# Small matmuls of the identity in the idle places of TensorE between two attentions

## The chip, the cores and the metric

The kernel runs on one core of one Trainium2 chip. The metric is the device time of one execution in microseconds, as the median of several runs.

## What is computed

The reference runs two layers over 16 batches of 512 queries with 256 channels, with a context of 1601 rows. Layer 0 is a masked cross attention with 16 heads of 16, an output projection, a residual and a layer norm. Layer 1 is a Mamba-2 block followed by a second cross attention (8 heads of 32) over the same context.

```python
def reference(x, ctx_1024, mask_BxSxS2_ik1, mask_1xS2_bf0, ...):
    x = _L0_xattn_ref(x, ctx_1024, ctx_1024, mask_BxSxS2_ik1, ...)
    x = _L1_xattn_ref(x, ctx_1024, mask_1xS2_bf0, ...)
    return x

# the Mamba-2 block of layer 1
zxbcdt = _rms(x, norm_w) @ in_proj_w
z, xBC, dt = ...
dt = jax.nn.softplus(zxbcdt[..., -H_M:] + dt_bias)
conv = conv_b + sum((padded[:, k:k + L, :] * conv_w[:, k] for k in range(D_CONV)))
xBC = jax.nn.silu(conv)
...
def step(h, inp):
    dec, u, bt, ct = inp
    h = h * dec[:, :, None, None] + u[..., None] * bt[:, None, None, :]
    y = jnp.einsum('bhpn,bn->bhp', h, ct)
    return (h, y)
...
u = _rms(y.reshape(b, L, D_INNER) * jax.nn.silu(z), gnorm_w)
return resid + u @ out_proj_w
```

## The kernel before

All engines run a loop over the 16 batches, each with its own list of instructions written out by hand, and they meet through semaphores (`s_...`). TensorE's loop body is the one that the change touches. In the order of its queue, one batch is:

1. `group(b, g)` for the four groups of heads of layer 0: scores (L975, L977, L979), probabilities times values (L1004), and, between them, the raw scores (`entry`, L941) of the next group, from which VectorE takes row maxima.
2. The output projection of layer 0 (`project_out`, L1123), with projections of layer 1's keys and values in between. These come from a list, `SECOND`; `fill(n)` takes the next n of them and calls `project` (L903). They write banks 6 and 7 of PSUM.
3. A wait for the layer norm and the RMS norm, which VectorE and GpSimd compute. Then eight transposes of `xs` (L1140) into banks 0 and 1, `fill(1)`, and a wait for `xn`, which ScalarE copies from the transposes.
4. The projection into the Mamba block: L1158 gives dt (16 matmuls with 8 columns), L1164 gives the channels, each with 512 columns. ScalarE copies each result (`copy_raw`), VectorE convolves it (L1701, L1705), ScalarE takes tanh, VectorE gates. The first `copy_raw` calls stand ahead of the exponential that VectorE's softplus waits for. `whole_decays` (L1089, L1090) and `window_sums` (L1081) write bank 4, and banks 4 and 5.
5. The scan over four windows of 128 positions: L1183, L1187, L1192, L1197, L1211, L1214, L1222, with one `fill(1)` in each. Bank 5 is read last by ScalarE's exponential into `Ce`, counted by `s_Ecb`.
6. The output projection of the block (`project_block`, L1226), the sums of squares (L1237: 32 matmuls with one column), `fill(3)`. A wait for the next layer norm, eight transposes of `xs1` (L1248) into banks 2 and 3, a wait for `xn`, and layer 1's q projection (`LASTQ`, L903).
7. SyncE copies q1 to its place by DMA (L558) while the context of the next batch is being loaded (`load_ctx`, L524). TensorE waits for this copy, then computes the raw scores of layer 1 (`entry1`, L960), with the first projections of the next batch in between, and the two groups of heads of layer 1.

An f32 matmul appears in the trace as two records, a bf16 one as a single record. Each record has a weight load beside it (PEld).

`identb` is the identity matrix in bf16, `ident` in f32. `s_rawfree` counts the raw scores of layer 0 that VectorE has read (banks 4 and 5), `NCOUNT` of them for a batch.

Of the kernel before, what the change touches and what calls it, by code (L numbers as in the profile page):

```python
# [51 lines left out]
def xattn_mamba(nc, x, xt, ctxt, mask, maskt, mask1, wq0, bq0, wk0, bk0, wv0, bv0, wo0, bo0, ln_g, ln_b,  # L52
# [4 lines left out]
    QT = T // P  # L57
# [15 lines left out]
    NCOUNT = G0 * (RAW + 1)  # L73
# [8 lines left out]
    LEAD = 1  # L82
# [7 lines left out]
    with ExitStack() as ctx:  # L90
        def sb(name, shape, dt):
            return ctx.enter_context(nc.sbuf_tensor(name, shape, dt))

        def sem(name):
            return ctx.enter_context(nc.semaphore(name))
# [24 lines left out]
        identb = sb("identb", [P, P], BF16)  # L120
# [117 lines left out]
        ps = ctx.enter_context(nc.psum_tensor("ps", [P, 8, 512], F32))  # L238
# [35 lines left out]
        s_rawfree = sem("s_rawfree")  # L274
# [45 lines left out]
        s_Ecb = sem("s_Ecb")  # L320
# [89 lines left out]
        for kind, _, _ in ENTRIES:  # L410
            counted.append(counted[-1] + (kind in ("raw", "turn")))
# [9 lines left out]
        for cuts in CUTS:  # L421
            at_slot = {}
            for lo, hi, t0, t1 in cuts:
                n = (t1 - t0 + 1) * SLOTS
# [447 lines left out]
        def _(pe):  # L872
# [4 lines left out]
            def project(b, item, bank, before):  # L877

                layer, kind, i = item
                if before is None:  # L880
                    pass
                elif before == (0, "v", before[2]):
                    pe.wait_ge(s_projfree, b * KT + before[2] + 1)
                elif before == (1, "v", before[2]):
                    pe.wait_ge(s_vfree, b * KT + before[2] + 1)
                else:
                    pe.wait_ge(s_rest, rests(b, before) + 1)
                for k in range(DT):
                    if kind == "q":
                        o = ps[:, bank, 0:T]  # L890
                        l = (wq0_s, wq1_s)[layer][:, k, i * P:(i + 1) * P]
                        r = (xt_s, xn)[layer][:, k, :]
                    elif kind == "k":
                        c, w = KCH[i[1]]
                        o = ps[:, bank, 0:w]
                        l = (wk0_s, wk1_s)[layer][:, k, i[0] * P:(i[0] + 1) * P]
                        r = ctxs[:, k, c:c + w]
                    else:
                        rows = P if i < KT - 1 else LAST
                        o = ps[0:rows, bank, 0:D]  # L900
                        l = ctxs[:, k, i * P:i * P + rows]
                        r = (wv0_s, wv1_s)[layer][:, k, :]
                    mm = pe.matmul(o, l, r, start=(k == 0), stop=(k == DT - 1))  # L903
                mm.then_inc(s_proj, 1)
# [196 lines left out]
            with pe.Fori(0, B) as b:  # L1101
# [7 lines left out]
                pe.wait_ge(s_wl, 16 * NRELOAD * (b + 1))  # L1109
                second = list(SECOND)  # L1110

                def fill(n):
                    for _ in range(n):
                        k = len(SECOND) - len(second)
                        item = second.pop(0)
                        project(b, item, pj_bank[item], SECOND[k - 2] if k >= 2 else None)
# [11 lines left out]
                pe.wait_ge(s_p, (b * NG + G0) * KT * 2)  # L1128
                project_out(wo0_s, 0, G0 - 1, G0, G0 - 1)
                fill(1)  # L1130
                pe.wait_ge(s_norm, LEAD + b * NG + G0)
                project_out(wo0_s, G0 - 1, G0, G0)
                fill(1)
                fill(NC - 2 + V_LN)

                pe.wait_ge(s_y, QT * (b + 1))
                for i in range(QT):
                    pe.wait_ge(s_xs, b * QT + i + 1)
# [1 line left out]
                        mm = pe.transpose(ps[:, k, i * P:(i + 1) * P], xs[:, i, k * P:(k + 1) * P], ident[:, :])  # L1140
                mm.then_inc(s_xst, 1)
                fill(1)
                pe.wait_ge(s_xn, DT * (b + 1))

                for j in range(1 + NCH + XT):
# [9 lines left out]
                    if j == 0:  # L1155
                        for i in range(QT):
                            for k in range(DT):
                                mm = pe.matmul(ps[:, bank, i * HM:(i + 1) * HM], xn[:, k, i * P:(i + 1) * P],  # L1158
                                               win_s[:, k, 2 * DI + 2 * NS:2 * DI + 2 * NS + HM],
                                               start=(k == 0), stop=(k == DT - 1))  # L1160
                    else:
                        c0 = DI + CORDER[j - 1] * P if j <= NCH else (j - 1 - NCH) * P
                        for k in range(DT):
                            mm = pe.matmul(ps[:, bank, :], win_s[:, k, c0:c0 + P], xn[:, k, :],  # L1164
                                           start=(k == 0), stop=(k == DT - 1))
                    mm.then_inc(s_in, 1)
                fill(V_IN)
                for c in range(QT):
# [24 lines left out]
                    if c > 0:  # L1193

                        pe.wait_ge(s_Ld, nb + 1)
                        for e in range(2):
                            mm = pe.matmul(ps[:, 4 + e, :], ones[:, :], aU[:, 4 * e:4 * e + 4, :],  # L1197
                                           start=True, stop=True)
# [36 lines left out]
                for i in range(QT):  # L1235
                    for k in range(XT):
                        mm = pe.matmul(ps[:, 4, i:i + 1], zs[:, k, i * P:(i + 1) * P], ones[:, 0:1],  # L1237
                                       start=(k == 0), stop=(k == XT - 1))
                mm.then_inc(s_op, 1)
                project_block(QT - 1)  # L1240
                fill(3)
                assert not second

                pe.wait_ge(s_blk, QT * (b + 1))
                for i in range(QT):
                    pe.wait_ge(s_xs1, b * QT + i + 1)
                    for k in range(DT):
                        mm = pe.transpose(ps[:, 2 + k, i * P:(i + 1) * P], xs1[:, i, k * P:(k + 1) * P], ident[:, :])  # L1248
                mm.then_inc(s_xst1, 1)
                pe.wait_ge(s_xn1, DT * (b + 1))  # L1250
                for item in LASTQ:
                    project(b, item, pj_bank[item], None)
# [2 lines left out]
                def forward():  # L1255
# [5 lines left out]
                        pe.wait_ge(s_vfree, (b + 1) * KT)  # L1261
                    project(b + 1, item, pj_bank[item], FRONT[n - 2] if n >= 2 else None)

                pe.wait_ge(s_q1, (b + 1) * DT)
                for n in range(NENT1):
                    entry1(b, n)
# [566 lines left out]
```

## Time and profile before

| | |
|---|---|
| median of 3 runs | 9563.34 us (9562.64 to 9577.86) |
| profiled execution | 9599.96 us |
| its span | 9597.9 us |
| busy: TensorE, VectorE, ScalarE, GpSimd | 84%, 52%, 35%, 20% |
| mean granted clock of TensorE | 0.880 |

The span is the time from the first to the last instruction of the profiled execution. A granted clock of 1.00 is 2.4 GHz and 0.50 is 1.2 GHz; TensorE has one or the other, and a mean between them says how long it had each. One batch takes about 585 us, so every place in the loop occurs 16 times.

### The profile page before, as it was taken

How to read it: one execution, taken by the hardware profiler on the slowest of the kernel's cores; microseconds unless marked ns; L12 is line 12 of the kernel's file. 1: busy time of each engine (PE TensorE's matmuls, PEld its weight loads, DVE VectorE, ACT ScalarE, POOL GpSimd, SP SyncE). 2: the span in 40 equal slices, each digit the busy share in tenths (PEclk: the TensorE clock that was granted, in tenths of full speed). 3: DMA queues.
4: the chain of work that ended last, by engine and by line, in shares of the span. 5: the costliest groups of instructions: out<-in, count | busy, mean ns of one | idle time of the engine just before them, and what ended most of it. 6: DMA issues, size and time to landing. Idle time of an engine off the chain costs nothing.

```text
span 9597.9 us, 129251 instructions
## 1 busy us (share of the span) xinstructions
PE 8034.6 (84%) x38020; PEld 3528.0 (37%) x38020; DVE 5004.5 (52%) x12781; ACT 3321.4 (35%) x4038; POOL 1965.2 (20%) x1798
## 2 busy tenths in 40 slices
PE   3979889798887979879798897988879788897987
PEld 1333433334333343433334333343333433334343
DVE  3456354554545555454553545545455554545545
ACT  0424334242342414324143242423424244241432
POOL 3030220302213031130311303022030221303113
PEclk6989889898898989889798898988989899897988
DMA  4132231312303132131322313223131320313223
GB/s 79 20 61 34 40 57 19 67 28 41 61 14 68 27 57 48 20 66 22 64 39 37 60 19 61 34 40 57 19 68 27 50 55 12 70 24 59 45 28 60
DMA packets 216597, 421.47 MB, mean 44 GB/s; under 512 B 35542, under 2 KB 126584, under 8 KB 215812
## 3 DMA queue, kind: packets, MB, share of 16 engines
q1 hardware_dynamic: 215889, 412.67, 25.4%
q8 instruction: 367, 6.01, 0.3%
q14 instruction: 341, 2.79, 0.1%
HBM read 190.14 MB, written 8.51 MB: 21 GB/s over the span
## 4 chain that ended last, share of the span: by engine, by line
PE 61%; issue 12%; DVE 10%; POOL 6%; DMA 5%; ACT 3%; SPq 2%; DVEq 0%; POOLq 0%; ACTq 0%
PE ps L1004 13%; PE ps L941 10%; PE ps L975 7%; PE ps L977 7%; PE ps L903 6%; PE ps L1009 4%; PE ps L979 3%; PE ps L1123 3%; DMA stage<-in_mask 3%; DVE mx L1577 3%; POOL maskq L693 2%; PE ps L960 2%; PE ps L1040 2%; DMA qst<-q1hl 1%; DVE xc L1705 1%
## 5 line engine op out<-in xcount | busy, mean ns | idle before, releaser
L1354 ACT ACTIVATE PR<-ps 128x1024 f32<-128x1024 f32 x2496 | 2501.9, 1024 | 3009.2 <-PE ps L977 1629.4
L1548 DVE CUSTOM_DVE_ANT_0 ps<-ps,maskq 128x402 f32<-128x402 f32 x4203 | 2408.4, 587 | 1929.8 <-PE ps L941 1399.4
L1004 PE MATMUL ps<-PR,vbuf 128*32 128x512 f32 x9984 | 1358.8, 617 | 5.1 <-ACT PR L1354 5.1
L977 PE MATMUL ps<-maskk,identb 128*128 128x512 bf16 x3328 | 1276.0, 383 | 0.0
L941 PE MATMUL ps<-kst,qst 96*128 96x402 bf16 (+1 forms) x3115 | 1028.6, 343 | 86.9 <-DVE mx L1548 71.5
L979 PE MATMUL ps<-qst,kst 102*128 102x512 f32 x1664 | 769.8, 527 | 391.7 <-DMA qst<-mrow 320.9
L1577 DVE TENSOR_REDUCE mx<-ps 128x2 f32<-128x804 f32 x1024 | 932.9, 985 | 187.6 <-PE ps L960 186.9
L975 PE MATMUL ps<-qst,kst 99*128 99x512 bf16 x2496 | 958.2, 384 | 0.0
L960 PE MATMUL ps<-kst,qst 100*128 100x402 f32 x2048 | 761.2, 499 | 228.3 <-DMA qst<-q1hl 127.6
L709 POOL TENSOR_TENSOR khl<-rest,khl 128x402 fp32r<-128x402 f32 (+1 forms) x128 | 123.6, 965 | 3442.8 <-ACT rest L1320 3442.8
L941 PEld LDWEIGHTS ps<-kst,qst 96*128 96x128 bf16 x3115 | 282.9, 97 | 1192.3 <-DVE mx L1548 804.0
L960 PEld LDWEIGHTS ps<-kst,qst 100*128 100x128 f32 x2048 | 420.9, 243 | 560.0 <-DVE mx L1577 377.3
L1548 DVE DVE_READ_ACCUMULATOR2_ANT mx<- 128x1 f32 x4203 | 590.7, 141 | 0.0
L941 PE MATMUL ps<-KS,QS 96*128 96x402 bf16 x1088 | 409.8, 377 | 167.3 <-DVE mx L1548 137.5
L979 PEld LDWEIGHTS ps<-qst,kst 102*128 102x128 f32 x1664 | 329.7, 206 | 544.4 <-issue 393.9
L1586 DVE RECIPROCAL rsm<-ps 128x128 f32<-128x128 f32 x80 | 76.6, 957 | 850.5 <-PE ps L1028 850.5
L693 POOL TENSOR_SCALAR maskq<-stage 128x402 bf16<-128x402 int32 (+1 forms) x272 | 426.1, 1566 | 438.8 <-DMA stage<-in_mask 427.7
L903 PE MATMUL ps<-ctxs,wk_s 128*128 128x402 f32 (+1 forms) x1056 | 458.5, 567 | 24.7 <-ACT rest L1320 23.7
L693 POOL TENSOR_SCALAR maskk<-stage 128x512 bf16<-128x512 int32 (+1 forms) x238 | 428.6, 1801 | 239.3 <-DMA stage<-in_maskt 231.0
L1009 PE MATMUL ps<-PR,ones 128*32 128x512 f32 x3328 | 453.4, 617 | 0.0
L903 PE MATMUL ps<-wv_s,ctxs 128*128 128x256 f32 (+1 forms) x1664 | 430.8, 395 | 9.3 <-ACT rest L1320 9.3
L977 PEld LDWEIGHTS ps<-maskk,identb 128*128 128x128 bf16 x3328 | 329.5, 99 | 266.6 <-issue 9.2
(194 smaller groups left out, 8044.2 us busy)
## 6 DMA issues: line engine op xcount, KB each, us to landing
kst<-khl SPq DMA_DIRECT2D x96, 800.5 KB, 16.1
kst<-khl SPq DMA_DIRECT2D x300, 200.1 KB, 7.6
stage<-in_maskt SPq DMA_DIRECT2D x204, 256.0 KB
stage<-in_mask SPq DMA_DIRECT2D x204, 201.0 KB
ctxs<-in_ctxt SPq DMA_DIRECT2D x17, 1601.0 KB, 13.6
qst<-q1hl SPq DMA_DIRECT2D x96, 256.0 KB, 7.7
win_s<-in_w_in SPq DMA_DIRECT2D x16, 1288.0 KB, 5.8
KS<-khl SPq DMA_DIRECT2D x102, 200.1 KB
```

Source lines behind the costliest of these rows:

```text
L693: nc.gpsimd.tensor_scalar(dst, stage[0:rows, n % 2, 0:w], 0.0, MASKED, ALU.is_equal, ALU.mult)\
L903: mm = pe.matmul(o, l, r, start=(k == 0), stop=(k == DT - 1))
L941: pe.matmul(ps[:, bank, 0:w], QS[gi][0:KROWS, h, i * P:(i + 1) * P], KS[gi][0:KROWS, h, c0:c0 + w], start=True, stop=True).then_inc(s_raw, 1)
L960: mm = pe.matmul(ps[:, bank + e, 0:CW], QS1[g][0:MROW1 + 1, h, i * P:(i + 1) * P], KS1[g][0:MROW1 + 1, h, cc[e]:cc[e] + CW], start=True, s ...
L975: pe.matmul(o, KS[gi][0:SROWS, h, t * P:(t + 1) * P], QS[gi][0:SROWS, h, :], start=True, stop=False)
L977: mm = pe.matmul(o, identb[:, :], maskk[:, t, :], start=False, stop=True)
L979: mm = pe.matmul(o, KS1[gi - G0][0:SROWS1, h, t * P:(t + 1) * P], QS1[gi - G0][0:SROWS1, h, :], start=True, stop=True)
L1004: mm = pe.matmul(ps[32 * j:32 * j + 32, 6, :], l, PR[:, t % 2, j, :], start=(t == 0), stop=(t == KT - 1), tile_position=(0, 32 * j))
L1009: mm = pe.matmul(ps[32 * j:32 * j + 32, 7, :], ones[:, 0:32], PR[:, t % 2, j, :], start=(t == 0), stop=(t == KT - 1), tile_position=(0, 32 ...
L1354: nc.scalar.activation(PR[:, t % 2, 2 * half:2 * half + 2, :], ps[:, 2 * half:2 * half + 2, :], ACT.Exp, scale=scale).then_inc(s_p, 1)
L1548: nc.vector.tensor_tensor_reduce(src, src, maskq[:, i, c0:c0 + w], 1.0, -3.0e38, ALU.add, ALU.max, mx[:, c, h * QT + i:h * QT + i + 1]).th ...
L1577: nc.vector.tensor_reduce(mx[:, 2 * c:2 * c + 2, h * QT + i], ps[:, bank:bank + 2, 0:CW], AX.X, ALU.max)\
```

## The change

In five places of the loop body TensorE issues small matmuls: the bf16 identity as weights, 64 columns of it as the moving operand, into the first 64 columns of PSUM bank 5, with nobody reading the result. There are 96 before the transposes of L1140, 16 after the `fill(1)` behind them, 64 before the transposes of L1248, 24 behind these, and 96 before the raw scores of layer 1. Two waits are added ahead of the first and third, for the last readers of bank 5.

```diff
@@ -1109,6 +1109,11 @@
                 pe.wait_ge(s_wl, 16 * NRELOAD * (b + 1))
                 second = list(SECOND)
 
+                def idle_work(n):
+
+                    for _ in range(n):
+                        pe.matmul(ps[:, 5, 0:64], identb[:, :], identb[:, 0:64], start=True, stop=True)
+
                 def fill(n):
                     for _ in range(n):
                         k = len(SECOND) - len(second)
@@ -1133,6 +1138,8 @@
                 fill(1)
                 fill(NC - 2 + V_LN)
 
+                pe.wait_ge(s_rawfree, LEAD + (b + 1) * NCOUNT)
+                idle_work(96)
                 pe.wait_ge(s_y, QT * (b + 1))
                 for i in range(QT):
                     pe.wait_ge(s_xs, b * QT + i + 1)
@@ -1140,6 +1147,7 @@
                         mm = pe.transpose(ps[:, k, i * P:(i + 1) * P], xs[:, i, k * P:(k + 1) * P], ident[:, :])
                 mm.then_inc(s_xst, 1)
                 fill(1)
+                idle_work(16)
                 pe.wait_ge(s_xn, DT * (b + 1))
 
                 for j in range(1 + NCH + XT):
@@ -1240,6 +1248,8 @@
                 project_block(QT - 1)
                 fill(3)
                 assert not second
+                pe.wait_ge(s_Ecb, (b + 1) * (QT - 1))
+                idle_work(64)
 
                 pe.wait_ge(s_blk, QT * (b + 1))
                 for i in range(QT):
@@ -1247,6 +1257,7 @@
                     for k in range(DT):
                         mm = pe.transpose(ps[:, 2 + k, i * P:(i + 1) * P], xs1[:, i, k * P:(k + 1) * P], ident[:, :])
                 mm.then_inc(s_xst1, 1)
+                idle_work(24)
                 pe.wait_ge(s_xn1, DT * (b + 1))
                 for item in LASTQ:
                     project(b, item, pj_bank[item], None)
@@ -1261,6 +1272,7 @@
                         pe.wait_ge(s_vfree, (b + 1) * KT)
                     project(b + 1, item, pj_bank[item], FRONT[n - 2] if n >= 2 else None)
 
+                idle_work(96)
                 pe.wait_ge(s_q1, (b + 1) * DT)
                 for n in range(NENT1):
                     entry1(b, n)
```

## Rows read from the trace of the kernel before

**Rows 1.** The page: the chain that ended last, by engine.

```profile
PE 61%; issue 12%; DVE 10%; POOL 6%; DMA 5%; ACT 3%; SPq 2%; DVEq 0%; POOLq 0%; ACTq 0%
```

**Rows 2.** Waits of TensorE, whole span: total us, times, longest.

```profile
PE ps L1140 <- DVE yt L1658: 132.1, 16, 8.5
PE ps L960 <- DMA qst<-q1hl: 127.6, 16, 10.7
...
PE ps L1248 <- DVE zs L1777: 61.8, 16, 4.5
```

**Rows 3.** Timeline of TensorE, two batches: start, us, what, times, idle before.

```profile
2815.79 1.94 PE L1140 MATMUL ps<-ident,yt 128*128 128x128 f32 x8 [8.25 <-DVE yt L1658]
...
2819.23 3.44 PE L1158 MATMUL ps<-win_s,xn 128*128 128x8 f32 x16
2822.52 13.51 PE L1164 MATMUL ps<-xn,win_s 128*128 128x512 f32 x24
...
2858.79 0.46 PE L1183 MATMUL ps<-xc 128*128 128x128 f32 x2 [2.66 <-DVE zs L1723]
...
2935.31 3.13 PE L960 MATMUL ps<-kst,qst 100*128 100x402 f32 x8 [7.26 <-DMA qst<-q1hl]
...
3395.84 1.94 PE L1140 MATMUL ps<-ident,yt 128*128 128x128 f32 x8 [8.24 <-DVE yt L1658]
...
3434.26 0.46 PE L1183 MATMUL ps<-xc 128*128 128x128 f32 x2 [1.98 <-DVE zs L1723]
...
3511.64 2.80 PE L960 MATMUL ps<-kst,qst 100*128 100x402 f32 x7 [8.48 <-DMA qst<-q1hl]
```

**Rows 4.** Stretches: busy us by engine (PE first), then PEclk, DMA share, GB/s.

```profile
534.60:536.80 2.20, 0.00 (x0) 0.02 (x1) 0.00 (x0) 1.00 (x3) 2.20 (x2) 1.00 0.00 0
...
560.70:563.00 2.30, 2.30 (x10) 1.95 (x10) 0.23 (x2) 0.00 (x0) 1.41 (x3) 0.79 1.00 111
...
2815.80:2827.00 11.20, 11.20 (x34) 8.07 (x35) 1.01 (x5) 2.25 (x4) 0.00 (x0) 0.50 0.85 93
...
3398.50:3407.00 8.50, 8.44 (x33) 4.72 (x32) 1.77 (x9) 2.28 (x6) 0.00 (x0) 1.00 0.79 87
```

**Rows 5.** Weight loads of two lines: times, ns min/median/max, first and last start.

```profile
L977 PEld LDWEIGHTS ps<-maskk,identb x3328: 95/98/152, 222.6 to 9208.2; 128*128 128x128 bf16 x196
...
L1237 PEld LDWEIGHTS ps<-ones,zs x512: 190/192/338, 557.0 to 9342.7; 128*128 128x128 f32 x171
```

**Rows 6.** Timeline of TensorE, matmuls in close sequence.

```profile
425.46 0.38 PE L975 MATMUL ps<-qst,kst 99*128 99x512 bf16 x1
425.68 0.38 PE L977 MATMUL ps<-maskk,identb 128*128 128x512 bf16 x1
...
550.51 0.44 PE L1211 MATMUL ps<-Ld,dx 128*64 128x128 f32 x4
550.73 0.44 PE L1214 MATMUL ps<-Ce,Hst 128*64 128x128 f32 x4
...
557.26 3.63 PE L1237 MATMUL ps<-ones,zs 128*128 128x1 f32 x32
```

**Rows 7.** Timeline of TensorE around L1248, first and second batch.

```profile
569.82 1.31 PE L1248 MATMUL ps<-ident,zs 128*128 128x128 f32 x8 [2.82 <-DVE zs L1777]
...
1156.60 1.94 PE L1248 MATMUL ps<-ident,zs 128*128 128x128 f32 x8 [4.51 <-DVE zs L1777]
1160.08 6.73 PE L903 MATMUL ps<-xn,wq_s 128*128 128x512 f32 x8 [1.54 <-ACT xn L1450]
```

**Rows 8.** Stretches around the copy of q1 (columns as in rows 4).

```profile
1164.00:1166.00 2.00, 2.00 (x3) 0.67 (x2) 0.75 (x1) 0.58 (x1) 1.30 (x1) 0.50 0.66 272
1166.00:1168.00 2.00, 0.81 (x2) 0.00 (x0) 0.43 (x1) 0.69 (x1) 0.30 (x1) 0.95 0.70 141
1168.00:1174.00 6.00, 0.00 (x0) 0.00 (x0) 0.32 (x1) 0.00 (x0) 0.00 (x0) 0.64 1.10 124
```

**Rows 9.** Timeline of SyncE's queue: the issue of the copies of q1.

```profile
1165.44 4.80 SPq L558 DMA_DIRECT2D qst<-q1hl  x6
```

## The prediction

> **What bounds the kernel now.** I read the page first, then the waits of TensorE, then the timeline and clock of the stretch that the change touches, once in every batch. TensorE is busy for 84% of the span, against 52% for VectorE, and it makes up 61% of the chain that ended last [rows 1]; its granted clock is 0.88 on average. So both its work and its clock count. The waits [rows 2] then show where it stands still in the stretch between the two attentions: 132.1 us before the transposes of L1140 (16 times, 8.26 us each), 61.8 us before those of L1248 (3.86 us each), and 127.6 us before L960 (7.97 us each). These are idle for a reason outside TensorE: VectorE and GpSimd compute a normalization, or a DMA lands. The idle time itself can't be filled with anything useful here. What can change is the clock at which the work behind it runs.
>
> The reader is to see two things in the first place [rows 3]. The transposes of L1140 run slowly (1.94 us for 8, where the scan has 4 of a like size every 0.22 us [rows 6]), and L1158 and the first L1164 follow without an idle mark. This work is on the path. VectorE waits for L1158 and for the copies of L1164, and from there on its convolution is what the scan waits for (2.66 us of idle time, ended by DVE zs, before L1183 [rows 3]). The price of a low clock is there as well: in the batch that starts its transposes at 2815.79 the scan starts 43.0 us later (2858.79), in the one at 3395.84 it starts 38.4 us later (3434.26). That is 4.6 us apart, of which 3.7 us are left at the first L960 (119.5 against 115.8 us). The difference is the clock: 0.50 in the 11 us after the transposes of the first, 1.00 from 2.7 us on in the second [rows 4]. Thirteen of the sixteen batches are nearer the first.
>
> **The change, part by part.** It adds 296 small matmuls a batch, 4736 in all, and two waits. Nothing is taken away and no DMA or other engine's instruction is added. The waits are for semaphores that were satisfied long before (the raw scores of the batch, and the last exponential of the scan), so they cost about nothing; what stands behind them on TensorE is the small work and then the transposes, and VectorE, ScalarE and the DMA of q1 wait for these in turn. Bank 5 has no reader at these points, so nobody waits for it to come free.
>
> Price of one pair of weight load and matmul (128 weights of bf16, 64 columns). The trace has no such pair. Lower end: matmuls of 512 columns of bf16 follow one another every 0.22 us [rows 6], their loads hidden behind them, so 64 columns would take an eighth, 30 ns, if their loads hid as well. Upper end: L1237 takes 3.63 us for 32 pairs with one column, 113 ns each; but those weights are f32. The nearest row is the scan's L1211 and L1214, 4 matmuls every 0.22 us, 55 ns each [rows 6], the closest spacing of loads and matmuls that lasts for 32 of them. I take 55 ns and keep 30 and 113 as ends.
>
> The Trainium skill ("TensorE: Matmul & The Clock Gate", section "Back-to-back issue gap") gives about 81 ns for a load and a matmul of 128 columns in a steady stream. No run here shows that figure. By it the third place would take 5.2 us where it has 3.86, and the work would be late in most batches; with 55 ns it is not.
>
> *First place, 96 before L1140:* 96 x 55 ns = 5.3 us, hidden in 8.26 us. It ends 3.0 us before the transposes. Does the clock last? After an idle stretch of 2.2 us in the scan it is still 1.00 [rows 4], after 4.51 us the transposes of L1248 run at 1.94 us, after 2.82 us at 1.31 [rows 7]. 3.0 us lies between, and these matmuls carry few columns for their time. I take it that the clock falls before the transposes as now in most batches, but that the moment moves so that it rises early in 6 batches and not 3: 3 x 3.7 us = 11 us gained.
>
> *Second place, 16 after the fill behind L1140:* there is no idle time before L1158 where the clock is low [rows 3], so 16 x 55 ns = 0.9 us is on the path, 16 times: 14 us lost. Cover exists only where the clock is high (the fill is then shorter than ScalarE's copies of xn).
>
> *Third place, 64 before L1248:* 3.5 us. Eleven batches have 4.51 us there and hide it, five have 1.93 to 2.83 us [rows 7], mean 2.44, and are late by 1.1 us: 5 us lost. *Fourth, 24 before the q projection:* 1.3 us in 1.54 us, hidden. These two should hold the clock: transposes of 1.94 would become 1.3 or less, and the first half of the q projection, which takes over half of the 6.73 us [rows 7], would take half. That is over 2 us, but what follows is a DMA. The copies of q1 are issued at 1165.44 [rows 9], when the load of the context is just over; the DMA engines are 66% and 70% busy in the two stretches of 2 us around it and full from 1168 on [rows 8]. So at most 0.68 + 0.60 = 1.3 us can be won; before that the queue is full. I take 1.0 us: 16 us gained.
>
> *Fifth place, 96 before L960:* 5.3 us, hidden in the 7.3 us or more before L960. Afterwards L960's consumer, VectorE, sets the pace of the raw scores; I count nothing. If the clock should last until then, only the first projection among them is quicker, about 1 us.
>
> Sum: -11 + 14 + 5 - 16 = -8 us. The profiled execution took 9599.96 us (span 9597.9, some 2 us around it), 37 us over the median of 9563.34; I carry the difference over to the median: 9555 us, which is within 0.2% (19 us), what a measurement of this kernel can tell from no change.
>
> **Rivals.** *The clock holds through the first place.* For it: the idle stretch left would have to be shorter by 0.8 us to be like the one of 2.2 us that the clock outlasts. Against it: the 3.6 us of one-column matmuls of L1237 [rows 6] are followed by a clock of 0.79 in the next 2.3 us, though TensorE is busy throughout [rows 4], so small matmuls need not count. Then up to 13 batches gain 3.7 us net, and the second place is mostly covered: 9563 - 48 + 5 - 16 = 9504 us; with the whole 4.6 us kept, 9492.
>
> *The pair costs more, and the small work makes the real work late.* One mechanism, the price of the pair, decides from 60 to 64 ns on (3.86/64, 1.54/24). At 80 ns: second place 16 x 1.3 = 20 us; third 5.1 us, 11 x 0.6 + 5 x 2.7 = 20 us; fourth 16 x 0.4 = 6 us; fifth 7.7 us, about 3 us; first still hidden (from 86 ns on it isn't); and little gain in clock: 9613 us. At 113 ns, L1237's price: 10.8 - 8.3 = 2.6, 1.8, 7.2 - 3.9 = 3.4, 2.7 - 1.5 = 1.2 and 10.8 - 8.0 = 2.9 us, together 11.9 us a batch, 190 us: 9753 us. Against this end: L1237's loads are f32, which take 192 ns where the bf16 ones take 98 [rows 5].
>
> *The small work does nothing to the clock,* as L1237 may suggest: only the second place's 14 us and the third's 5 us remain, 9582 us.
>
> **How the numbers follow.** Chances: the forecast's case (a pair of 40 to 60 ns, clock gained only in places 3 and 4) 0.54; clock held through the first place 0.20; pair around 80 ns 0.11; pair around 113 ns 0.10; nothing to the clock 0.05. The forecast's own range is 9530 to 9585, since in which batch the clock rises early is partly luck, 4 us each. It gives faster 0.15, same 0.33, slower 0.06. With the others: faster 0.15 + 0.20 = 0.35; same 0.33 + 0.03 (a pair only a little dear, or no effect) = 0.36; slower 0.29. The range of 9480 to 9630 takes in the first rival and the 80 ns and leaves out the 113 ns and a little below, under 0.2.
>
> **What would show it.** Of the pair: the distance of the new matmuls in the timeline (55 ns), and where the first place ends, 3.0 us before L1140. Of the clock: eight transposes of L1140 in 1.94 us (as now) or near 0.95; L1248 at 1.3 or less in most batches; the q projection at 3.6 to 5.1 us. Of the path: L1158 begins 0.9 us later behind the transposes where the clock is low; the idle time before L960 grows by what q gained over 1.3 us. I am wrong if the idle mark before L1140 or L1248 is gone (the pair is dear), or if the scan starts 38 us after L1140 in most batches (the clock held).

## The result: slower by 0.74%, and the profile after

The changed kernel takes 9637.8 us (median; 9603.04 to 9655.55) against 9562.99: ratio 1.0074, 95% interval 1.0041 to 1.0107. Timed again beside later runs it was 1.0089 (1.0069 to 1.0110). The forecast was no change (9555 us, range 9480 to 9630), so it is wrong. The profiled execution after is the fastest of its runs, 9603.04 us, and that of before (9599.96) took longer than any of its timed runs; so the two spans are nearly equal, and stretches are compared below, not spans. A mean over the sixteen batches is always that of one profiled execution.

The waits of TensorE after (same columns as [rows 2]; L1147, L1258 stand for the L1140, L1248 of before):

```profile
PE ps L960 <- DMA qst<-q1hl: 159.1, 16, 12.5
...
PE ps L1147 <- DVE yt L1670: 87.1, 16, 5.6
```

The wait before the transposes of L1147 fell from 132.1 to 87.1 us, 5.4 us each: the first place ends 5.4 us before them, and not 3.0 as predicted. The wait for the copy of q1 *rose* by 31.5 us, although 96 small matmuls now stand in it. The timeline of TensorE, the same batch as the first of [rows 3]:

```profile
2800.30 2.96 PE L1115 MATMUL ps<-identb 128*128 128x64 bf16 x96
2808.69 1.94 PE L1147 MATMUL ps<-ident,yt 128*128 128x128 f32 x8 [5.43 <-DVE yt L1670]
2810.43 1.66 PE L903 MATMUL ps<-wv_s,ctxs 128*128 128x256 f32 x4
2811.92 0.63 PE L1115 MATMUL ps<-identb 128*128 128x64 bf16 x16
2812.39 1.71 PE L1166 MATMUL ps<-win_s,xn 128*128 128x8 f32 x14
2815.13 0.39 PE L1166 MATMUL ps<-win_s,xn 128*128 128x8 f32 x2 [1.03 <-issue]
...
2911.52 1.31 PE L1258 MATMUL ps<-ident,zs 128*128 128x128 f32 x8 [0.26 <-DVE zs L1789]
...
2914.38 3.70 PE L903 MATMUL ps<-xn,wq_s 128*128 128x512 f32 x8 [0.84 <-ACT xn L1462]
...
2931.06 5.51 PE L960 MATMUL ps<-kst,qst 100*128 100x402 f32 x13 [10.18 <-DMA qst<-q1hl]
```

A pair costs 29 ns: (2.96 - 0.19)/95, where 0.19 is one matmul's own duration. The transposes of L1147 still take 1.94 us, in all batches. The q projection is quick, 3.70 us in every batch, against 5.10 to 6.77 before (mean 6.06). Yet L960 starts 19.5 us after L1258, where before it was 2935.31 [rows 3] - 2917.81 = 17.5 in this batch:

```profile
2917.81 1.94 PE L1248 MATMUL ps<-ident,zs 128*128 128x128 f32 x8 [4.51 <-DVE zs L1777]
2921.29 6.76 PE L903 MATMUL ps<-xn,wq_s 128*128 128x512 f32 x8 [1.54 <-ACT xn L1450]
```

SyncE's queue says why, after first:

```profile
2910.03 0.38 SPq L524 DMA_DIRECT2D ctxs<-in_ctxt  x1
2917.95 3.91 SPq L558 DMA_DIRECT2D qst<-q1hl  x6
```

and before, same batch:

```profile
2913.94 0.38 SPq L524 DMA_DIRECT2D ctxs<-in_ctxt  x1
2926.66 4.84 SPq L558 DMA_DIRECT2D qst<-q1hl  x6
```

The copies are issued 7.9 us behind the load of the context, and not 12.7. From issue to L960 they take 13.1 us, where before it was 8.7. The stretches after (columns as in rows 4) show the two transfers share the DMA engines:

```profile
2914.00:2918.00 4.00, 3.62 (x11) 1.62 (x12) 0.75 (x1) 1.01 (x2) 1.89 (x2) 1.00 1.04 386
2918.00:2922.00 4.00, 2.88 (x97) 2.75 (x95) 0.75 (x1) 0.69 (x1) 1.57 (x2) 1.00 1.08 242
```

The first stretch, at 386 GB/s, has the load of the context and not yet the copies; from the moment the copies join, the rate falls to 242, while the engines stay full. Over the sixteen batches the timeline gives, from the issue of the copies to L960, 8.8 us before and 12.9 after; and the load takes 13.1 us before and 15.7 after.

### The profile page after: what moved, and what is told of

Read it like the earlier page. It is cut to its first block, busy times and chain, and to the rows that moved or that the text cites. A ratio compares the mean times of both kernels' runs of the same rounds, so it can differ in the third digit from the quotient of the medians.

```text
span 9601.0 us, 138419 instructions
## 1 busy us (share of the span) xinstructions
PE 8075.4 (84%) x42436; PEld 3653.2 (38%) x42756; DVE 5008.8 (52%) x12781; ACT 3325.1 (35%) x4038; POOL 1963.4 (20%) x1798
## 4 chain that ended last, share of the span: by engine, by line
PE 59%; issue 13%; DVE 10%; POOL 6%; DMA 6%; SPq 3%; ACT 2%; DVEq 0%; POOLq 0%; ACTq 0%
PE ps L1004 12%; PE ps L941 10%; PE ps L975 7%; PE ps L977 6%; PE ps L903 6%; PE ps L1009 3%; PE ps L979 3%; DMA stage<-in_mask 3%; PE ps L1128 3%; DVE mx L1589 3%; POOL maskq L693 2%; DMA qst<-q1hl 2%; PE ps L960 2%; PE ps L1040 2%; SPq L537 1%
## 5 line engine op out<-in xcount | busy, mean ns | idle before, releaser
L977 PE MATMUL ps<-maskk,identb 128*128 128x512 bf16 x3008 | 1149.5, 382 | 0.0
L960 PE MATMUL ps<-kst,qst 100*128 100x402 f32 x2048 | 754.3, 497 | 263.3 <-DMA qst<-q1hl 159.1
L960 PEld LDWEIGHTS ps<-kst,qst 100*128 100x128 f32 x2048 | 422.8, 243 | 571.9 <-DVE mx L1589 383.1
```

What stands on the lines that cost most here:

```text
L960: mm = pe.matmul(ps[:, bank + e, 0:CW], QS1[g][0:MROW1 + 1, h, i * P:(i + 1) * P], KS1[g][0:MROW1 + 1, h, cc[e]:cc[e] + CW], start=True, s ...
L977: mm = pe.matmul(o, identb[:, :], maskk[:, t, :], start=False, stop=True)
```

## The experiments

Ratios are to the kernel before, with 95% intervals; us are medians, so a ratio can differ a little from that of the two medians beside it. Places are numbered one to five as in the diff.

| run | median, before beside it | ratio |
|---|---|---|
| third and fourth place only | 9600.33, 9556.36 | 1.0039 (1.0025 to 1.0053) |
| first and fifth only | 9564.61, 9556.36 | 1.0005 (0.9993 to 1.0018) |
| change, copies of q1 held | 9638.09, 9556.36 | 1.0089 (1.0067 to 1.0111) |
| third and fourth, copies first | 9526.93, 9556.36 | 0.9965 (0.9950 to 0.9979) |
| copies first, no small matmuls | 9562.64, 9569.86 | 0.9996 (0.9981 to 1.0011) |
| second only, 64 matmuls | 9596.11, 9569.86 | 1.0030 (1.0017 to 1.0044) |
| first only, 264 matmuls | 9740.06, 9569.86 | 1.0186 (1.0161 to 1.0211) |
| first with 264, third, fourth, copies first | 9674.89, 9569.86 | 1.0117 (1.0095 to 1.0138) |
| first only, 35 wide | 9547.06, 9550.21 | 0.9997 (0.9984 to 1.0011) |
| first wide, third, fourth, copies first | 9488.81, 9550.21 | 0.9937 (0.9918 to 0.9956) |
| change without second | 9595.77, 9550.21 | 1.0059 (1.0039 to 1.0078) |
| change again | 9629.85, 9550.21 | 1.0089 (1.0069 to 1.0110) |
| second only | 9612.32, 9555.27 | 1.0076 (1.0052 to 1.0099) |
| change, copies first | 9586.73, 9555.27 | 1.0040 (1.0025 to 1.0055) |
| second only, 2 wide | 9585.76, 9555.31 | 1.0038 (1.0021 to 1.0056) |
| second only, again | 9610.09, 9555.31 | 1.0060 (1.0039 to 1.0082) |

**Third and fourth place only.** The other three calls and the first wait are left out.

> Only the third and fourth places (64 before L1248, 24 behind it). Theory 1, collision of transfers: the clock is held, the q projection takes 3.7 us where it took 6.06, its copy is issued some 2 us earlier and meets the load of the context, so that it lands 12 to 13 us after its issue and not 8.8; the first L960 starts 1 to 2 us later behind L1248 than before, and the kernel is 15 to 35 us slower than before. Theory 2, the cost lies in the second place and in when the clock changes: the third and fourth places alone gain, the copy takes 8.8 us as before, and the kernel is 15 to 35 us faster.

1.0039, 44 us slower, and 12.8 us from the issue of the copies to L960. From L1248's transposes to L960 it takes 19.6 us in the mean, against 17.3 before: 2.2 us a batch, 36 of the 44 us. The q projection is quick and still costs time: the collision is at work without any other part of the change.

**First and fifth only.**

> Only the first and fifth places (96 each). Both theories: they lie in idle time, take 2.8 us each, end 5 us or more before the next real matmul, and change nothing: within 10 us of before, L1140 still at 1.94 us for its eight transposes, the copy of q1 at 8.8 us. A third theory, that the changed moments of the clock are what costs: 20 to 60 us slower, with the copy of q1 at 8.8 us.

1.0005: together they cost and win nothing that the timed runs can tell. The trace has a small cost of the fifth place all the same. The instruction queue of the DMA engines (q8 in the DMA view) moves 383 packets in this kernel and 367 before: one block of 16 KB of instructions more in each batch, and it falls among the copies of q1. In five batches it starts 2.5 us behind their issue, and L960 starts 9.5 to 9.7 us behind it; in the other eleven it starts 6.7 us behind or later, and L960 starts at 8.6 to 8.7. So an early block goes with 1.0 us of delay, 5 us in this kernel.

**Third and fourth place, copies of q1 first.** The same small matmuls, and the order of two transfers turned round, which needs TensorE's wait for the context at a later projection (the first two read only x):

```diff
                 sp.wait_ge(s_vfree, (b + 1) * KT)
                 alone(sp)
-                load_ctx(bn)
                 for g in range(G1):
                     stack_q1(b, g)
+                load_ctx(bn)
...
                     if n == 0:
                         pe.wait_ge(s_xt, 16 * (b + 2))
+                    if n == DT:
                         pe.wait_ge(s_ctx, 16 * (b + 2))
+                    if n == 0:
                         pe.wait_ge(s_vfree, (b + 1) * KT)
```

> The third and fourth places, and SyncE issues the copies of q1 ahead of the load of the context; TensorE waits for the context at the third projection of the next batch, the first that reads it, and no longer at the first. Theory 1: without a load beside it the copy lands 7 to 8.7 us after its issue, the first L960 starts 4 to 6 us earlier behind L1248 than in the kernel before, and the load is over by the third projection: 50 to 90 us faster than before. Theory 2: the copy takes 8.8 us as before: 30 to 50 us faster. If the later context or mask loads become a wait, less or none of it is left.

0.9965. SyncE's queue and TensorE's timeline of this kernel:

```profile
2914.83 3.89 SPq L558 DMA_DIRECT2D qst<-q1hl  x6
2918.90 0.46 SPq L524 DMA_DIRECT2D ctxs<-in_ctxt  x1
```

```profile
2907.79 1.94 PE L1255 MATMUL ps<-ident,zs 128*128 128x128 f32 x8 [2.64 <-DVE zs L1787]
...
2911.26 3.70 PE L903 MATMUL ps<-xn,wq_s 128*128 128x512 f32 x8 [0.41 <-ACT xn L1460]
2923.49 5.84 PE L960 MATMUL ps<-kst,qst 100*128 100x402 f32 x14 [8.53 <-DMA qst<-q1hl]
```

8.7 us from issue to L960, and 15.7 from the transposes; the means are 8.7 and 15.6, where before had 8.8 and 17.3. The collision is gone and the quick projection wins 1.75 us a batch, 28 us. In size it is theory 2 that holds (the copy takes what it took before, 30 to 50 us faster; measured 29 in the medians, 33 by the ratio), and theory 1's 50 to 90 us are a miss: a copy that meets no load is no quicker than it was before.

**Copies first, without small matmuls.**

> No small matmuls at all, only the order of the transfers: the copies of q1 ahead of the load of the context, and TensorE's wait for the context moved to the third projection. Theory 1 (the copy takes 8.7 us whenever no load stands beside it, and took 8.8 before): the order alone changes nothing, within 12 us of before; the 29 us that the third and fourth places won in this order are theirs. Rival, that the order itself was the gain: 20 to 40 us faster.

0.9996: the order alone wins nothing. What it does is to let the quick projection be worth something.

**The whole change, copies of q1 held** until the load has landed: `sp.wait_ge(s_ctx, 16 * (b + 2))` ahead of them.

> The whole change, and SyncE waits until the load of the context has landed before it issues the copies of q1. Theory 1: the copy then takes 8.7 us from its issue again, the load of the context lands within 10.3 to 13.7 us of its issue where the change had 15.7, and in spite of the later issue the first L960 starts about 1 us earlier than with the change alone, so 10 to 20 us faster than the change (9615 to 9628). Theory 2: the hold is a pure delay of 2 to 5 us a batch, 30 to 80 us slower than the change.

The same as the change, 1.0089 both. The copies take 8.65 us again, but they start at 12.4 us behind the load's issue, not 8.2, and L960 starts 21.0 us behind it in both. The expectation of 10 to 20 us was a miss: a load of 12.2 us and then copies of 8.65 end where the two end that share the engines. Making the copies wait wins nothing; putting them first does.

**The whole change, copies first.**

> The whole change, with the copies of q1 issued ahead of the load of the context and TensorE's wait for the context at the third projection. If the collision is what the third and fourth places cost, the copies take 8.7 us again, and the kernel is 50 to 70 us faster than the change: within 15 us of before with the second place's cost at 10 us, up to 25 us slower than before if that place costs 30. If the collision is not the cause: 60 us or more slower than before.

1.0040, 43 us under the change timed again (in ratios 1.0040 against 1.0089), and still 31 us over before. So the collision is about half of the loss. The expected 8.7 us of the copies did not come true either:

```profile
2922.12 3.90 SPq L558 DMA_DIRECT2D qst<-q1hl  x6
2932.02 5.84 PE L960 MATMUL ps<-kst,qst 100*128 100x402 f32 x14 [6.97 <-DMA qst<-q1hl]
```

That is 9.9 us, and 9.7 in the mean, where the third and fourth places alone had 8.7 in this order. It is what the first-and-fifth kernel showed: in 14 of the 16 batches the block of instructions starts 4.5 to 4.8 us behind the issue of the copies, and L960 comes 9.7 to 9.9 us behind it; in one it starts at 6.7 us, and L960 comes at 8.9. The kernel with the third and fourth places alone has no such block there. So 1.0 us a batch, 16 of the 31 us, goes with the fifth place, and most likely with its instructions. But one batch of each of these two kernels has 9.6 us without a block among the copies, so the block is not the only thing that delays them, and no run takes it away alone.

**The change without its second place, and the change again.**

> The change without its second place. If the second place costs what its quadruple suggests (0.3% for 64, so about 7 us for 16) on top of 14 us of path time at most, this is 7 to 20 us faster than the change and 9 to 30 us slower than third and fourth alone (9600), so 9605 to 9630. If the second place is what the change loses beyond the third and fourth, it is 9595 to 9608.

> The change itself, timed again beside these: 50 to 90 us slower than before.

1.0059 against 1.0089: 34 us for the second place, more than the 7 to 20 expected. The 9595.77 us lie in the other expectation's 9595 to 9608, that the second place is what the change loses beyond the third and fourth.

**The second place alone,** with 16 matmuls, twice, with 64, and with 2 of 512 columns.

> Only the second place, 16 matmuls as in the change. If it costs its path time (0.6 us between the transposes and L1158 in the change's trace), it is 5 to 15 us slower than before. If the moved moments of the clock cost as well, 25 to 40 us slower.

> The 16 small matmuls of the second place alone, once more: 35 to 75 us slower than before if the first result holds, 15 to 30 if it was chance and the truth is near that of the 64.

> Only the second place, with 64 matmuls in place of 16. Theory: they stand on the path between the fill and L1158, at 54 ns each while the clock is low (3.5 us) and 29 ns where it is high (1.9 us), less the cover by ScalarE's copies; L1158 starts 2 to 3 us later behind the transposes, and the kernel is 25 to 50 us slower than before. Rival, that the dense columns lift the clock sooner and pay for themselves: within 15 us of before.

> Second place alone, with 2 matmuls of 512 columns in place of 16 of 64: 0.85 us at low clock, as the 16 take. If the delay, with the moments of the clock that it moves, is the cost: 35 to 70 us slower than before, as p2. If only the path time counts: 5 to 15 us slower. If it is the small form (few columns for its time, or 28 more instructions): less than half of what p2_again shows.

16 cost 0.76% and 0.60%, the first above both of its expected ranges; 64 cost 0.30%; 2 wide ones 0.38%, less than the 16 but not less than half. In the trace of the first, where the clock is low:

```profile
470.30 1.91 PE L903 MATMUL ps<-wv_s,ctxs 128*128 128x256 f32 x4
472.01 1.06 PE L1115 MATMUL ps<-identb 128*128 128x64 bf16 x16
472.88 3.56 PE L1165 MATMUL ps<-win_s,xn 128*128 128x8 f32 x16
```

A pair takes (1.06 - 0.26)/15 = 53 ns there, and L1165 starts 4.31 us behind the transposes (468.57) and not 3.44 [rows 3]. Over the batches that is 0.75 us, 12 us in all. The 64 put 2.7 us on the path, but the work behind them runs at the high clock (the 16 records of L1158 in 1.93 us and not 3.16), and the eighth record of L1164 ends 11.5 us behind the transposes' start, against 12.3.

The path time of the 16 is 12 us. More can be read from the traces, from the start of the transposes of L1140 to the end of L1237, in the mean of the sixteen batches. Six kernels have no second place and no first place longer than the change's: before, first and fifth, third and fourth in both orders, copies first, and the change without its second. Six have the 16 small matmuls:

| kernels | mean, us | batches of 96 us or more |
|---|---|---|
| the six without | 91.4 to 92.7 | 0 of 96 |
| the six with the 16 | 93.3 to 94.5 | 40 of 96 |
| 2 wide | 93.4 | 5 of 16 |
| 64 | 93.0 | 0 of 16 |

The means of the two sixes are 92.2 and 93.9 us: 1.7 us a batch, 27 us, of the 34 to 73 that the second place costs in medians and ratios. In the 40 long batches of these kernels the scan starts 43.4 to 43.6 us behind the transposes, and the clock is 0.50 for 3.4 us between 84.3 and 88.0 us, from the end of the scan into the matmuls ahead of L1237, where TensorE is busy. Without the second place the scan never starts later than 43.1 us, and in no batch does this happen. With the 64 it starts at 41.6 us or earlier, no batch is long, and they cost less than the 16. So half a microsecond of delay goes with a low clock in another place. A matmul form of its own does not explain the cost, since 2 wide ones cost 30 us as well.

**The first place alone, filled up:** `idle_work(264)`, 7.7 us at 29 ns.

> Only the first place, with 264 matmuls and not 96: 264 x 29 ns = 7.7 us of the 8.24 us of idle time. If the clock can be held through this place, the eight transposes of L1140 take about 1.0 us and not 1.94, the q-side work up to the eighth L1164 about 7.5 us and not 12.3, and the scan starts 38 to 41 us behind L1140 in all batches (mean before 45.5): 50 to 80 us faster. If matmuls of this form don't hold it, the transposes stay at 1.94 us, nothing is won, and if the clock falls while they run (54 ns each) the place ends late by up to 6 us: 0 to 90 us slower.

1.0186, twice the worst that was expected. Timeline and waits of TensorE:

```profile
459.37 4.25 PE L1115 MATMUL ps<-identb 128*128 128x64 bf16 x140
473.73 5.27 PE L1115 MATMUL ps<-identb 128*128 128x64 bf16 x124 [10.11 <-issue]
478.84 0.53 PE L1147 MATMUL ps<-ident,yt 128*128 128x128 f32 x3
```

```profile
PE ps L1115 <- issue: 162.5, 16, 10.8
```

TensorE stands still for 10.1 us in the middle of its own small matmuls, and "issue" says that it waits for nothing that the profile shows. In all sixteen batches it stops behind the 140th. The DMA view has more. From 455 to 469 us, first fence, the copies of the keys fill the DMA engines and no packet of the instruction queue is moved; the next half microsecond from 469.9, second fence, has it (queue, packets, MB, share). It has landed 1.7 us before TensorE goes on:

```profile
q1 hardware_dynamic: 264, 1.59, 95.4%
issues: line engine op xcount, KB each, median us to landing
kst<-khl SPq DMA_DIRECT2D x3, 800.5 KB, 17.4
```

```profile
q8 instruction: 1, 0.02, 23.9%
```

**The same with the copies first, and third and fourth place.**

> First place with 264, third and fourth as in the change, none in the second and fifth, the copies of q1 ahead of the load of the context. The sum of the parts: 29 us faster by the order with the third and fourth places, and 50 to 80 us by the first if it holds the clock: 9430 to 9480 in all. If the first doesn't hold it: 9527 or slower.

1.0117: the same idle time of 10 us in every batch, less what the other parts win.

**The first place with few instructions.** 35 matmuls of 512 columns, the same time in 70 instructions and not 528:

```diff
+                def wide_work(n):
+                    for _ in range(n):
+                        pe.matmul(ps[:, 5, :], identb[:, :], identb[:, :].unsqueeze(1).broadcast_to([P, 4, P]), start=True, stop=True)
...
-                idle_work(96)
+                wide_work(35)
```

> Only the first place, with 35 matmuls of 512 columns (the 128 columns of the identity four times over) in place of 264 of 64 columns: the same 7.6 us at full clock, with 70 instructions and not 528. Theory A, instructions ran out: the 10.1 us of idle time in the middle of the 264 was TensorE waiting for its next block of instructions behind the copies of the keys; with 70 instructions there is no such gap, the clock holds, L1140 takes 1.0 us, the scan starts 38 to 41 us behind it, and the kernel is 40 to 75 us faster than before. Theory B, the clock or the waits themselves are at fault (the place waits for something that comes late): the gap is there again, 10 us a batch, and the kernel is 150 us slower. Under A it could still be less than 40 us if the scan loses what the projection wins.

```profile
2777.97 7.72 PE L1120 MATMUL ps<-identb 128*128 128x512 bf16 x35
2786.39 1.13 PE L1152 MATMUL ps<-ident,yt 128*128 128x128 f32 x8 [0.70 <-DVE yt L1670]
...
2788.88 1.95 PE L1170 MATMUL ps<-win_s,xn 128*128 128x8 f32 x16 [0.49 <-ACT xn L1395]
...
2824.00 0.46 PE L1195 MATMUL ps<-xc 128*128 128x128 f32 x2 [1.30 <-DVE zs L1735]
```

There is no idle time inside the work, so the 10 us went with the number of instructions, as theory A had it. The transposes take 1.13 us in all batches, L1170 1.95 us, and the scan starts 37.6 us behind the transposes; its mean is 37.9 over the batches, against 41.9 before. That, too, is what theory A said. Yet the time is the same, 0.9997, where 40 to 75 us were expected. Between the profile of this kernel and that of the first-and-fifth one (spans 9538.9 and 9562.2) the stretch up to the scan is 3.8 us a batch shorter; 0.6 us are given back from the end of the scan to the end of L1237, at a lower clock, 0.4 between L1248 and L960, and 1.2 in the stretches of the two attentions. So over half is given back, and the profiles keep 1.5 us a batch, of which the timed runs show nothing clear. Between L1248 and L960 part of it is the collision again, without the third and fourth places: in four of the 16 batches the copies of q1 are issued 10.1 to 10.4 us behind a load that takes 15.6 to 18.0 us, and from issue to L960 they take 11.5 to 14.0 us where the other twelve have 8.5 to 9.3. That is 18 us in all.

**All that helped together:** the first place wide, third and fourth as in the change, copies first.

> The first place with 35 matmuls of 512 columns, third and fourth as in the change, the copies of q1 ahead of the load of the context. Theory A: the gains add, 70 to 105 us faster than before, 9455 to 9490. Theory B: slower than before.

0.9937 (0.9918 to 0.9956), 61 us faster than before. That is 9 us short of the least that was expected, and yet more than the two parts won when each was timed alone (29 and 3 us in the medians), though the intervals hardly separate the two. The trace has a reason for it: with the copies first, no batch collides, and all sixteen have 8.6 to 8.7 us from their issue to L960. So the first place wide, which won nothing alone, may win something once the copies go first; the timed runs don't settle it.

## Why the prediction was wrong

- **Price of the pair, 55 ns: wrong.** 29 ns at the high clock, 53 at the low one; the lower end that was kept, 30, was right. The row of the same type, bf16 with its loads hidden, gave it. The row that was taken, the scan's, is another thing: its four records in 0.22 us are two f32 matmuls of two records each, with loads of 64 columns, and they run side by side on two halves of the array (`tile_position=(0, 64 * e)`). The 32 records of L1237 are 16 matmuls, too. The Trainium skill ("TensorE: Matmul & The Clock Gate", section "Back-to-back issue gap") gives about 81 ns for a load and a matmul of 128 columns; by it the third place would have been late, an estimate that the trace of these matmuls of 64 columns does not bear out, since it never was.
- **First place, 11 us gained: not there.** With 29 ns the work ends 5.4 us early, the clock falls as before (1.94 us in all batches), and first and fifth together change nothing that the timed runs can tell. The rival "the clock holds" was possible: a place filled to 0.7 us of its end does hold it. Alone it won far less than the 3.7 us a batch that two batches of one trace had suggested.
- **Third and fourth, 16 us gained: the step that failed.** The clock was held as said and the q projection won more than foreseen (the first half takes 1.98 us, not 3.64). But "at most 1.3 us can be won; before that the queue is full" treated an earlier issue into a full queue as free. It costs: the copies, issued 9.7 us behind the load in the mean and not 11.7, take 12.8 us and not 8.8, and L960 comes 2.2 us a batch later. These two places alone were measured at +44 us in place of -16, and at -29 where the copies go first. The rows showed the load of the context ending just as the copies were issued; the question not asked was what the copies would do to the load, and it to them.
- **Second place, 14 us lost: right in its path time, too small in its effect.** 0.75 us a batch in the trace, 0.9 as worked out; 34 to 73 us in the timed runs. This term is too small by a factor of two and a half to five. It counted only the path time; up to the end of L1237 the traces have 27 us, path time included.
- **Fifth, nothing: nearly right.** The matmuls are hidden. But L960 came 1.0 us later where an early block of instructions lay among the copies, in five batches of one kernel and in 14 of another (5 and 16 us), and the prediction had no term for instructions. **Third place late by 5 us:** it was not, the work took 1.9 us.
- **The range** ended at 9630, 8 us short of the measured median. Its upper end was set by a dear pair, which was not the cause, and no case had the transfers collide.

What stays open: the rest of the second place's cost, 7 to 46 us beside the 27, which is as wide as the timed runs leave it, and why half a microsecond of delay goes with a low clock in another place. That the delay brings it about is argued from which batches have it. It was not tried to delay the same point without TensorE working.

## What to carry to other kernels

Work that makes an engine faster ahead of a transfer also starts the transfer earlier: look what else is in the DMA engines at the new time of issue, and put the transfer that is waited for ahead of the one that is not (here 73 us between the two orders, +44 and -29). To keep TensorE's clock up through this wait, the work had to reach nearly to its end (0.7 us before it held the clock, 5.4 us did not), and with few, wide matmuls (35 wide ones had no stop, 264 small ones had 10 us), since blocks of instructions come through the same DMA engines as the data. A batch of one trace that happened to run quicker is no measure of what its cause is worth to the whole.

## What the runs showed of the hardware

- A matmul of 64 columns in bf16 with a load of 128 columns: every 29 ns at 2.4 GHz, for 96 in a row; every 53 ns at 1.2 GHz, for 16 in a row.
- TensorE stopped for 10.1 us after 140 such pairs, in every batch, while the copies of the keys filled the DMA engines, and went on after a block of instructions had landed; 35 wide matmuls in the same place had no stop. That the copies held the block up, and not that it was asked for late, no run separates. In the changed kernel the same may be seen in small: 6.1 us in 8 batches before L1166 (1.03 us in the timeline above), in the same stretch of full DMA engines.
- Copies that need 8.7 us from issue to first use took 12.9 when issued 8.2 us behind a load (mean of 16 batches), which itself went from 13.1 to 15.7 us.
- A block of 16 KB of instructions that starts 2.5 to 4.8 us behind the issue of these copies goes with 1.0 us more from issue to first use; one that starts at 6.7 us does not (five against eleven batches of the first-and-fifth kernel, 14 batches of the change with the copies first).
